# A four-layer token mixer on one core: the comparison of layer 4's weights moves into layer 2's attention and onto GpSimd

## The chip, the cores and the metric

The kernel runs on one core of a Trainium2 chip. The metric is the time of one execution on the device in microseconds, and a kernel is represented by the median of its runs. The engines are named as in the profile: PE (TensorE, with PEld for its weight loads), DVE (VectorE), ACT (ScalarE), POOL (GpSimd) and SP (SyncE, which issues the transfers).

## The reference

Four sequences of 1024 tokens with 256 features pass through four blocks, each followed by a residual sum and a layer norm. The change touches the second block, here called layer 2:

```
q, k   = x @ w_q, x @ w_k                       # 8 heads of 64
gates  = sigmoid(x @ w_gate)                    # 8 experts for each head
gm     = one_hot(argmax(gates)) * gates         # one expert per token and head
values = einsum('bhne,ehdk,bnd->bhnk', gm, value_experts, x)
attn   = softmax(causal(q k^T / 8))
out    = einsum('bhne,ehkd,bhnk->bhnd', gm, output_experts, attn @ values).sum(heads)
```

Layer 4 is a gated feed-forward network whose weights (w1, w2, h1, h2, w3; 128 x 22528 numbers in the layout on the chip) come from the inputs. The kernel copies them to `weights_copy` in DRAM and compares, while layer 2 runs, each number with its value rounded to fp32r. The largest difference goes to `misfit`, and layer 4 leaves out its low-order products where that is zero.

## The kernel before, in words

Layer 2 (`layer2`, line 458) loops over the four sequences, and each turn has three stages, each a block of instructions that all engines finish before the next begins: `values()`, `attention(own, b)` and `output_experts(own, b)`. Engines are synchronised by semaphores. The order on each engine is written out by hand: a number (a tick in the attention, a block in the output stage) runs in the code of every engine, and tables say what happens at which number.

**Attention.** Ticks x run from 8 to 82, eight to a head. In tick x, PE computes the scores of key tile k2 of one head (L902 to L905) into three banks in turn, perhaps a projection (`project`, L659), then the maxima product of query tile k1 of a later head (L886, L888), and last the product of the probabilities with the values of the tick before (L913). ACT takes the exponentials (L944), copies a head's result out (`head_out`, L951) and takes the high parts of a projection (`hi_parts`, four copies). DVE takes the row maxima (L976; the width falls from 1024 to 128 columns over the eight ticks) and then, where a projection stands in the tick, its low parts (`lo_parts`). A pair of heads needs four projections (`parts`: k, k, q, q), which share one bank, so that each waits for the low parts of the one before. In the first five tiles of a head, the maxima product of a tile waits for the row maximum of the tile before. POOL divides six heads by their denominators (L999), which SP carries there and back through DRAM. SP also carries each row maximum to the row that the scores read.

**Output stage.** 64 blocks i (head pair c, expert e, half n; 16 blocks for one c) go through a chain: PE spreads the gates of the block (`mask`, L627), DVE multiplies (`route`, L635), ACT takes the high part (`route_hi`, L642), POOL the low part (`route_lo`, L648), and three blocks later PE does the twelve products (L1176). A ring of four tiles holds the routed blocks. Between these, by number of the block: ACT and DVE split the output experts of the next c into high and low parts (`split_at`; ACT at i, DVE at i + 2), the next sequence is normalised (statistics at block 5, `SD_AT`, `NORM_FROM`, scaling in the eight blocks behind), turned (`turn_at`), its gate logits computed (`LOGITS_AT`, L537) and the gates worked out in ten steps (`GATES_FROM`). The comparison of the weights stands here too: 16 pieces of 128 x 352, each fetched by SP, rounded by ACT (L1103), compared by DVE (L1147) and reduced by DVE (L1152).

## Time and profile before

| what | value |
|---|---|
| runs | 3595.15, 3596.03, 3611.57 us; median 3596.03 |
| the profiled execution | 3602.37 us, span 3600.7 us |
| mean granted clock of TensorE | 0.955 |
| layer 2, four sequences | from 356.2 to about 2004 us |
| PE busy over the span | 3239.3 us (90%) |
| DVE, ACT, POOL busy | 1953.9, 1509.1, 842.4 us |

A row of the timeline gives the start in us, the duration, the engine, the line, the operation with its tiles and shape, how many instructions are merged, and in brackets how long the engine had been idle and what released it. A row of the windows gives the stretch and its length, then the busy time of PE, PEld, DVE, ACT and POOL with the number of instructions, then the granted clock of TensorE (1.00 is 2.4 GHz, 0.50 is 1.2 GHz), the DMA share and GB/s. A row of the groups gives busy us and the mean in ns of one instruction, then the idle time before them and its releaser. The four sequences of layer 2 look alike almost to the tenth of a microsecond, so rows of the first one stand for all.

### The profile page before, as it was taken

What the parts mean: (1) busy time and instruction counts of PE and PEld (TensorE: products, weight loads), DVE (VectorE), ACT (ScalarE), POOL (GpSimd) and SP (SyncE); (2) the same over time, 40 slices, a digit from 0 to 9 for tenths busy, and PEclk for the clock granted to TensorE, in tenths of its full rate; (3) what the DMA queues carried; (4) which work ended last, traced back from release to release, by engine and by line L of the source; (5) the groups of instructions that cost most, each with busy time, mean ns of one, the idle gap of its engine ahead of it and who ended that gap; (6) DMA issues with size and microseconds to landing.
All of it is one profiled execution on the core that took longest, in us unless ns stands there. A gap on an engine that the chain in (4) does not pass through costs nothing. (4 is left out here: it accounts for less than half of the span.)

```text
span 3600.7 us, 50745 instructions
## 1 busy us (share of the span) xinstructions
PE 3239.3 (90%) x18306; PEld 2331.5 (65%) x18306; DVE 1953.9 (54%) x3377; ACT 1509.1 (42%) x2795; POOL 842.4 (23%) x753
## 2 busy tenths in 40 slices
PE   7895999889988999889989698998989979999998
PEld 4554755876568755777558554646556468888887
DVE  4344843867458654677439374765747533333332
ACT  2331144422444134431544455474655634444443
POOL 1121511653037411554027300101000011111111
PEclk9897999999999999999999899999999989999999
DMA  5111100210021100211012101000010030000000
GB/s 190 47 35 66 30 19 13 91 43 24 10 59 49 48 15 16 83 46 30 10 43 64 48 2 26 1 2 25 2 25 2 14 160 12 13 18 12 7 6 12
DMA packets 189927, 127.33 MB, mean 35 GB/s; under 512 B 125808, under 2 KB 174192, under 8 KB 186224
## 3 DMA queue, kind: packets, MB, share of 16 engines
q1 hardware_dynamic: 189680, 124.02, 12.2%
q8 instruction: 157, 2.57, 0.3%
q14 instruction: 90, 0.74, 0.1%
HBM read 106.52 MB, written 28.44 MB: 37 GB/s over the span
## 5 line engine op out<-in xcount | busy, mean ns | idle before, releaser
L1610 ACT ACTIVATE l3b_prob<-sums 128x512 f32<-128x512 f32 (+3 forms) x768 | 332.9, 494 | 207.3 <-PE sums L1543 168.3
L648 POOL TENSOR_TENSOR l_qrow<-l_vm,l_qst 128x512 fp32r<-128x512 f32 x256 | 364.0, 1435 | 205.8 <-ACT l_qst L642 187.0
L1859 PE MATMUL sums<-l_uhi,l_h 128*128 128x512 f32 x1024 | 409.1, 399 | 0.0
L1859 PE MATMUL sums<-l_ulo,l_h 128*128 128x512 f32 x1024 | 403.1, 394 | 0.0
L976 DVE TENSOR_REDUCE l2b_mx<-sums 128x1 fp32r<-128x1024 f32 (+7 forms) x256 | 192.6, 758 | 301.1 <-PE sums L888 299.4
L944 ACT ACTIVATE sb_nx<-sums 128x512 f32<-128x512 f32 (+3 forms) x384 | 181.9, 492 | 355.8 <-PE sums L905 351.2
L913 PE MATMUL sums<-sb_nx,l_vx 128*128 128x512 f32 (+3 forms) x768 | 302.4, 503 | 13.0 <-ACT l_od L951 13.0
L1538 PE MATMUL sums<-l_qst,l_kst 64*128 64x512 f32 (+3 forms) x768 | 276.3, 426 | 21.5 <-DMA l_qst<-l3b_peak 10.9
L1945 DVE TENSOR_TENSOR l_ulo<-l_made,l_uhi 128x512 fp32r<-128x512 f32 x128 | 90.5, 707 | 362.1 <-ACT l_uhi L1876 362.0
L642 ACT CAST l_qst<-l_vm 128x512 fp32r<-128x512 f32 x256 | 157.4, 619 | 240.0 <-DVE l_vm L635 239.6
L1521 PE MATMUL sums<-l_kst,l_qst 64*128 64x512 f32 (+3 forms) x768 | 237.6, 431 | 20.6 <-DVE l3b_low L1622 11.4
L1538 PEld LDWEIGHTS sums<-l_qst,l_kst 64*128 64x128 f32 x768 | 140.3, 195 | 159.0 <-ACT l3b_prob L1610 143.0
L736 PE MATMUL sums<-l_kst,l_qst 128*128 128x512 f32 x512 | 211.2, 412 | 34.5 <-issue 20.6
L635 DVE TENSOR_TENSOR l_vm<-l_oT,sums 128x512 f32<-128x512 f32 x256 | 170.6, 679 | 124.2 <-PE sums L627 123.6
L772 DVE TENSOR_TENSOR l_vm<-sums,l_gm 128x512 f32<-128x512 f32 x256 | 175.0, 689 | 95.2 <-PE sums L736 94.6
L1176 PE MATMUL sums<-l_kst,l_qst 128*128 128x256 f32 x768 | 225.1, 293 | 0.0
L1859 PEld LDWEIGHTS sums<-l_uhi,l_h 128*128 128x128 f32 x1024 | 192.5, 188 | 47.7
L1859 PEld LDWEIGHTS sums<-l_ulo,l_h 128*128 128x128 f32 x1024 | 192.6, 188 | 42.9
L902 PE MATMUL sums<-l_qst,l_kst 128*128 128x512 f32 (+3 forms) x384 | 209.0, 544 | 0.0
L1904 ACT ACTIVATE l_made<-sums,l_scale 128x512 f32<-128x512 f32 x128 | 88.1, 688 | 279.8 <-PE sums L1859 279.7
L736 PE MATMUL sums<-l_kst,l_qrow 128*128 128x512 f32 x512 | 202.6, 396 | 0.0
L736 PE MATMUL sums<-l_krow,l_qst 128*128 128x512 f32 x512 | 202.4, 395 | 0.0
(270 smaller groups left out, 7870.8 us busy)
## 6 DMA issues: line engine op xcount, KB each, us to landing
l_ve<-ve SPq DMA_DIRECT2D x34, 512.0 KB, 4.1
l_oe<-oe SPq DMA_DIRECT2D x16, 1024.0 KB, 6.3
l_vm<-weights_copy SPq DMA_DIRECT2D x64, 176.0 KB, 2.3
sb_nx<-between SPq DMA_DIRECT2D x9, 1024.0 KB, 5.6
weights_copy<-h SPq DMA_DIRECT2D x2, 4096.0 KB, 26.6
l_ve<-inverse SPq DMA_DIRECT2D x32, 256.0 KB, 3.6
l_qst<-l3b_peak SPq DMA_DIRECT2D x512, 0.5 KB, 2.0
l_h<-weights_copy SPq DMA_DIRECT2D x2, 4096.0 KB, 23.6
```

Source lines behind the costliest of these rows:

```text
L648: pool.tensor_tensor(rlo[:, i % RT, :], routed[:, i % RT, :], rhi[:, i % RT, :].bitcast(F32), ALU.subtract).then_inc(s3.routed_lo, 1)
L736: last = pe.matmul(bank(m.ps, n % RING), x[:, c, t * P:(t + 1) * P], v[:, h % 2, c, :], start=(c == 0 and x is xhi and v is vhi), stop=(c ...
L772: dve.tensor_tensor(by_key(vm[:, n % VM, :]), by_key(bank(m.ps, n % RING)), gm[:, at:at + NE].unsqueeze(1).to_broadcast([P, DH0, NE]), ALU ...
L902: pe.matmul(out, kst[:, h % RK, at], qst[:, h % RK, lo:hi], start=True, stop=False)
L913: last = pe.matmul(bank(m.ps, PV, lo, hi), vx[:, k, h // 2, DH0 * (h % 2):DH0 * (h % 2) + P], prob[:, k % 2, lo:hi], start=(k == 0), stop= ...
L944: act.activation(prob[:, k % 2, lo:hi], bank(m.ps, n % 3, 0, hi - lo), ACT.Exp, scale=SCALE0).then_inc(s.exp_ready, 1)
L976: dve.reduce_max(mx[:, h1, t:t + 1], bank(m.ps, max_bank(h1, k1), 0, (t + 1) * P), AX_X).then_inc(s.max_read, 1)
L1176: last = pe.matmul(m.ps[:, t * D:(t + 1) * D], r[:, k % RT, cols], w(c, expert(e))[:, 0, :], start=(c == e == 0 and t % 2 == 0 and r is rh ...
L1521: last = pe.matmul(bank(m.ps, at, 0, hi - lo), qst[rows(a), p, t * P:(t + 1) * P], kst[rows(a), p, lo:hi], start=True, stop=True)
L1538: last = pe.matmul(bank(m.ps, part % SCORE, 0, hi - lo), kst[rows(a), p, k * P:(k + 1) * P], qst[rows(a), p, lo:hi], start=True, stop=True)
L1610: act.activation(prob[:, i % RB, j, a, 0:hi - lo], bank(m.ps, part % SCORE, 0, hi - lo), ACT.Exp, scale=SCALE1).then_inc(s.exp_ready, 1)
L1859: run(lambda out, a, x, first, last: pe.matmul(out, a, x, start=first, stop=last))
```

## The change

- **Comparison.** It leaves the output stage for the attention. There are now eight pieces of 128 x 704 in a sequence. SP fetches two ahead and one more in the second tick of heads 1 to 6; POOL rounds (a cast) and subtracts; DVE takes the result into `worst` by one instruction (not_equal, then max) at the seventh tick of heads 1 to 8. ACT has no part in it. `worst` is reduced to `misfit` once, at the end of the layer. The pieces lie in the tile `vm`, which the attention doesn't use before its last ticks.
- **Projections.** They start at tick 1 of a pair of heads instead of tick 2, so that they stand at odd ticks (k1 = 1, 3, 5, 7) and not at even ones (2, 4, 6, and 0 of the next head).
- **Split of the second pair's output experts.** Blocks 9 and 13 instead of 4 and 8.
- **Statistics.** Four parts of two tiles at blocks 4 to 7, the moments at block 8, where all stood at block 5; the root and the scaling begin two blocks later, as do turns, logits and gates. The last divisions begin one block earlier.

```diff
+    CHECKS = 8
+    W = m.weights_copy.shape[1] // (SEQS * CHECKS)
+    scratch = vm[:, :, :].rearrange("p a n -> p (a n)")
+    word = scratch[:, 0:2 * W].rearrange("p (a n) -> p a n", a=2)
+    rounded, unlike = scratch[:, 2 * W:3 * W].bitcast(F32R), scratch[:, 3 * W:4 * W]
+    worst = sb("worst", [P, W])
...
         WAIT = 2
-        APART = 2
+        PROJECT_FROM, APART = 1, 2
...
         def project_in(x):
-            c, ahead = divmod(x - WAIT, 2 * NT)
+            c, ahead = divmod(x - PROJECT_FROM, 2 * NT)
             if 1 <= c < H0 // 2 and ahead in range(0, 4 * APART, APART):
                 return c, ahead // APART
...
                 sp.dma_start(oe[:, :, :], I["oe2"][:, 0]).then_inc(s.oe_in, 16)
+                sp.wait_ge(m.weights_copied, 16 * len(WEIGHTS4))
+                for j in range(2):
+                    weight_chunk(j)
                 for h in range(H0):
                     if h >= 2:
                         sp.wait_ge(carried[h % 2], carried_to(h - 2))
@@ -856,6 +872,9 @@
                         sp.dma_start(qrow[DH0:ROWS, h % RK, t * P:(t + 1) * P].bitcast(F32),
                                      mx[:, h, t:t + 1].bitcast(F32)).then_inc(carried[h % 2], 16)
                         over = h - 2
+                        if 1 <= h <= CHECKS - 2 and k == CHUNK_AT:
+                            sp.wait_ge(s.weight_unlike, h)
+                            weight_chunk(h + 1)
...
@@ -976,6 +995,9 @@
                         dve.reduce_max(mx[:, h1, t:t + 1], bank(m.ps, max_bank(h1, k1), 0, (t + 1) * P), AX_X).then_inc(s.max_read, 1)
                     if project_in(x):
                         lo_parts(dve, *project_in(x))
+                    if k1 == NT - 2 and h1 >= 1:
+                        dve.wait_ge(s.weight_unlike, h1)
+                        dve.scalar_tensor_tensor(worst[:, :], unlike, 0.0, worst[:, :], ALU.not_equal, ALU.max).then_inc(s.weight_taken, 1)
...
                 pool.memset(krow[DH0:ROWS, :, :].bitcast(F32), -1.0).then_inc(s.row_ready, 1)
+                step = Chain(pool, s.weight_chain)
+
+                def check_weights(j):
+                    pool.wait_ge((s.even_weight_in, s.odd_weight_in)[j % 2], 16 * (j // 2 + 1))
+                    step(pool.tensor_copy(rounded, word[:, j % 2, :]))
+                    if j:
+                        pool.wait_ge(s.weight_taken, j)
+                    pool.tensor_tensor(unlike, word[:, j % 2, :], rounded.bitcast(F32), ALU.subtract).then_inc(s.weight_unlike, 1)
+                    pool.wait_ge(s.weight_unlike, j + 1)
+
+                pool.wait_ge(s.row_ready, 1)
+                check_weights(0)
+                check_weights(1)
                 for h in range(DIVIDED):
+                    if h:
+                        pool.wait_ge(s.o_ready, h)
+                    check_weights(h + 2)
                     pool.wait_ge(s.rden_in, 16 * (h + 1))
                     pool.tensor_tensor(oT[vcol(h), h // 2, :], od[vcol(h), h % 2, :], rden[vcol(h), :], ALU.mult).then_inc(s.o_ready, 1)
...
-        turn_at = {11 + 3 * t: t for t in range(NT)}
-        x_hi_at = {12 + 3 * t: t for t in range(NT)}
-        x_lo_at = {13 + 3 * t: t for t in range(NT)}
-        LOGITS_AT, GATES_FROM, EXP_AT, STATS_AT, SD_AT, NORM_FROM = 35, 37, 38, 5, 6, 7
-        LAST_TURNED, last_o_at = 4, {24: (6, 0), 27: (6, 1), 30: (7, 0), 33: (7, 1)}
-        VALUE_HI_AT, value_lo_at = 48, {49: 0, 51: 1}
+        turn_at = {13 + 3 * t: t for t in range(NT)}
+        x_hi_at = {14 + 3 * t: t for t in range(NT)}
+        x_lo_at = {15 + 3 * t: t for t in range(NT)}
+        LOGITS_AT, GATES_FROM, EXP_AT, MOMENTS_AT, SD_AT, NORM_FROM = 37, 39, 40, 8, 8, 9
+        stats_at = {4: 0, 5: 1, 6: 2, 7: 3}
+        LAST_TURNED, last_o_at = 4, {23: (6, 0), 26: (6, 1), 29: (7, 0), 32: (7, 1)}
+        VALUE_HI_AT, value_lo_at = 51, {53: 0, 55: 1}
         PER_C = NE * NH
         oe_in = (None, s3.oe_in1, s3.oe_in2, s3.oe_in3)
-        split_at = {4: (1, 0), 8: (1, 1)}
+        split_at = {9: (1, 0), 13: (1, 1)}
         split_at.update({(c - 1) * PER_C + 4 + 4 * j: (c, j) for c in range(2, H0 // 2) for j in range(2)})
...
-        CHECKS = 16
-        W = m.weights_copy.shape[1] // (SEQS * CHECKS)
-        word = vm[:, RT:VM, 0:W]
-        rounded = sb("rounded", [P, 2, W], F32R)
-        worst = sb("worst", [P, CHECKS + 1])
-        check_at = {8 + 3 * j: j for j in range(CHECKS)}
-        weight_in = (s3.even_weight_in, s3.odd_weight_in)
...
-                def weight_chunk(j):
-                    if j >= 2:
-                        sp.wait_ge(s.weight_checked, j - 1)
-                    sp.dma_start(word[:, j % 2, :],
-                                 m.weights_copy.rearrange("p (b j n) -> b j p n", b=SEQS, n=W)[b, j]).then_inc(weight_in[j % 2], 16)
...
-                sp.wait_ge(m.weights_copied, 16 * len(WEIGHTS4))
-                for j in range(4):
-                    weight_chunk(j)
                 for c in range(2, H0 // 2):
                     sp.wait_ge(s.oe_lo, 2 * c)
                     sp.dma_start(oe[:, :, :], I["oe2"][:, c]).then_inc(oe_in[c], 16)
-                    for j in range(6 * c - 8, 6 * c - 2):
-                        weight_chunk(j)
                     if c == 2:
                         sp.wait_ge(s.last_o_ready, len(last_o_at))
                         for h in range(2):
@@ -1095,12 +1116,6 @@
...
-                    if i in check_at:
-                        j = check_at[i]
-                        act.wait_ge(weight_in[j % 2], 16 * (j // 2 + 1))
-                        if j >= 2:
-                            act.wait_ge(s.weight_compared, j - 1)
-                        act.copy(rounded[:, j % 2, :], word[:, j % 2, :]).then_inc(s.weight_rounded, 1)
...
-                    if i == STATS_AT:
-                        fetch_stats(dve, m, sf)
+                    if i in stats_at:
+                        part = stats_at[i]
+                        if part == 0:
+                            dve.wait_ge(sf.nx_in, 16)
+                        for t in range(2 * part, 2 * part + 2):
+                            stat = dve.bn_stats(m.stats[:, t, :], m.nx[:, t, :])
+                        stat.then_inc(sf.nx_stats, 1)
+                    if i == MOMENTS_AT:
+                        dve.wait_ge(sf.nx_stats, len(stats_at))
+                        for t in range(NT):
+                            moment = dve.bn_aggr(m.moments[:, t, :], m.stats[:, t, :])
+                        moment.then_inc(sf.nx_moments, 1)
...
-                    if i - 1 in check_at:
-                        j = check_at[i - 1]
-                        dve.wait_ge(s.weight_rounded, j + 1)
-                        dve.wait_ge(weight_in[j % 2], 16 * (j // 2 + 1))
-                        dve.tensor_tensor(word[:, j % 2, :], word[:, j % 2, :], rounded[:, j % 2, :].bitcast(F32),
-                                          ALU.not_equal).then_inc(s.weight_compared, 1)
-                    if i - 2 in check_at:
-                        j = check_at[i - 2]
-                        dve.wait_ge(s.weight_compared, j + 1)
-                        dve.reduce_max(worst[:, j:j + 1], word[:, j % 2, :], AX_X).then_inc(s.weight_checked, 1)
-                dve.wait_ge(s.weight_checked, CHECKS)
-                dve.reduce_max(worst[:, CHECKS:], worst[:, 0:CHECKS], AX_X).then_inc(s.worst, 1)
-                dve.wait_ge(s.worst, 1)
-                dve.tensor_tensor(m.misfit[:, :], m.misfit[:, :], worst[:, CHECKS:], ALU.max).then_inc(s.worst, 1)
                 for t in range(NT):
                     dve.wait_ge(s.out_mm, len(blocks) - (t < NT // 2))
                     dve.tensor_tensor(m.x[:, t, :], m.x[:, t, :], m.ps[:, t * D:(t + 1) * D], ALU.add).then_inc(s.y_ready, 1)
...
+        @block.vector
+        def _(dve):
+            dve.reduce_max(m.misfit[:, :], worst[:, :], AX_X)
```

On DVE in the attention, the rows of the last two projections of a pair (`lo_parts` of the q halves, with the row maxima around them). Before:

```order
L976 TENSOR_REDUCE l2b_mx<-sums 128x1
L982 RECIPROCAL l_denp<-l_denp 128x8
L976 TENSOR_REDUCE l2b_mx<-sums 128x1
L686 TENSOR_TENSOR l_qrow<-sums,l_qst 64x512 x2
L976 TENSOR_REDUCE l2b_mx<-sums 128x1 x2
L686 TENSOR_TENSOR l_qrow<-sums,l_qst 64x512 x2
L976 TENSOR_REDUCE l2b_mx<-sums 128x1 x5
```

Of the changed kernel, at the same place:

```order
L693 TENSOR_TENSOR l_qrow<-sums,l_qst 64x512 x2
L1004 RECIPROCAL l_denp<-l_denp 128x8
L995 TENSOR_REDUCE l2b_mx<-sums 128x1
L1000 SCALAR_TENSOR_TENSOR l_worst<-l_vm,l_worst 128x704
L995 TENSOR_REDUCE l2b_mx<-sums 128x1
L693 TENSOR_TENSOR l_qrow<-sums,l_qst 64x512 x2
L995 TENSOR_REDUCE l2b_mx<-sums 128x1 x6
```

The last low parts stood behind the first row maximum of the next head and now stand ahead of it, and the new `worst` instruction stands between the last two maxima of the head.

On DVE at the start of the output stage, from the third route on. Before:

```order
L635 TENSOR_TENSOR l_vm<-l_oT,sums 128x512 x2
L1124 RECIPROCAL l_denp<-l_denp 128x16
L635 TENSOR_TENSOR l_vm<-l_oT,sums 128x512
L126 BN_STATS sb_stats<-sb_nx 128x6 x8
L130 BN_AGGR sb_moments<-sb_stats 128x2 x8
L1114 TENSOR_TENSOR l_kst<-l_oe,l_krow 128x1024
L635 TENSOR_TENSOR l_vm<-l_oT,sums 128x512 x2
L112 RECIPROCAL sb_rstd<-sb_sd 128x8
```

Of the changed kernel:

```order
L1145 BN_STATS sb_stats<-sb_nx 128x6 x2
L642 TENSOR_TENSOR l_vm<-l_oT,sums 128x512
L1145 BN_STATS sb_stats<-sb_nx 128x6 x2
L642 TENSOR_TENSOR l_vm<-l_oT,sums 128x512
L1145 BN_STATS sb_stats<-sb_nx 128x6 x2
L642 TENSOR_TENSOR l_vm<-l_oT,sums 128x512
L1145 BN_STATS sb_stats<-sb_nx 128x6 x2
L642 TENSOR_TENSOR l_vm<-l_oT,sums 128x512
L1150 BN_AGGR sb_moments<-sb_stats 128x2 x8
L642 TENSOR_TENSOR l_vm<-l_oT,sums 128x512
L112 RECIPROCAL sb_rstd<-sb_sd 128x8
```

The statistics come between the routes in pairs, the low part of an expert half (L1114 before) is gone from here, and the reciprocal of the root follows four routes later.

On POOL in the attention, from the memset of the score rows on. Before, the memset (L996) was followed by the divisions of heads alone. Of the changed kernel:

```order
L1018 MEMSET l_krow 1x4096
L1023 CAST l_vm<-l_vm 128x704
L1026 TENSOR_TENSOR l_vm<-l_vm 128x704
L1023 CAST l_vm<-l_vm 128x704
L1026 TENSOR_TENSOR l_vm<-l_vm 128x704
L1023 CAST l_vm<-l_vm 128x704
L1026 TENSOR_TENSOR l_vm<-l_vm 128x704
L1037 TENSOR_TENSOR l_oT<-l_od,l_ve 64x1024
```

Three pieces are rounded and subtracted ahead of the first head's division (the last row), and one piece stands ahead of each further one.

## Rows read from the trace of the kernel before

**Rows 1.** View by windows, output stage of the first sequence.

```profile
629.00:765.00 136.00, 119.58 (x877) 113.99 (x877) 106.76 (x162) 57.61 (x105) 88.89 (x63) 0.95 0.22 70
```

**Rows 2.** View of waits, 629 to 765 us (us in total, times, longest).

```profile
PE sums L1176 <- POOL l_qrow L648: 11.8, 7, 4.3
```

**Rows 3.** Timeline of PE, output stage; in brackets the idle time before.

```profile
631.11 0.47 PE L627 MATMUL sums<-l_gmT,l_sel 128*128 128x512 f32 x1 [3.17 <-PEq L844]
644.04 0.55 PE L1176 MATMUL sums<-l_ohi,l_qst 128*128 128x256 f32 x1 [4.26 <-POOL l_qrow L648]
721.60 0.55 PE L1176 MATMUL sums<-l_ohi,l_qst 128*128 128x256 f32 x1 [2.59 <-POOL l_qrow L648]
754.79 0.40 PE L627 MATMUL sums<-l_gmT,l_sel 128*128 128x512 f32 x1
756.46 0.40 PE L627 MATMUL sums<-l_gmT,l_sel 128*128 128x512 f32 x1
```

**Rows 4.** Windows with the granted clock (PEclk), three stretches.

```profile
644.00:650.00 6.00, 5.96 (x27) 5.85 (x28) 3.31 (x7) 4.05 (x7) 4.12 (x4) 0.53 0.24 65
721.00:725.00 4.00, 3.40 (x16) 3.34 (x17) 3.93 (x5) 1.19 (x2) 2.10 (x3) 0.57 0.00 0
516.00:520.00 4.00, 4.00 (x14) 1.95 (x12) 0.74 (x1) 1.36 (x3) 0.00 (x0) 1.00 0.04 3
```

**Rows 5.** Groups of instructions by line, 629 to 765 us.

```profile
L648 POOL TENSOR_TENSOR l_qrow<-l_vm,l_qst 128x512 fp32r<-128x512 f32 x63 | 89.6, 1435 | 41.7 <-ACT l_qst L642 37.0 <-PE sums L1176 4.6
L635 DVE TENSOR_TENSOR l_vm<-l_oT,sums 128x512 f32<-128x512 f32 x61 | 40.6, 678 | 18.5 <-PE sums L627 18.4
L642 ACT CAST l_qst<-l_vm 128x512 fp32r<-128x512 f32 x61 | 37.6, 620 | 59.9 <-DVE l_vm L635 59.8
L1147 DVE TENSOR_TENSOR l_vm<-l_vm,l2c_rounded 128x352 f32<-128x352 f32 x16 | 20.4, 1273 | 2.7 <-ACT l2c_rounded L1103 2.3
L537 PE MATMUL sums<-l_wg,l_xT 128*128 128x64 f32 x32 | 3.7, 273 | 0.0
```

**Rows 6.** Timeline of DVE and ACT, blocks 4 to 7.

```profile
637.93 2.71 DVE L126 BATCH_NORM_STATS2 sb_stats<-sb_nx 128x6 f32<-128x256 f32 x8 [0.78 <-DMA sb_nx<-between]
640.45 1.04 ACT L1081 CAST l_krow<-l_oe 128x1024 fp32r<-128x1024 f32 x1 [7.49 <-DMA l_oe<-oe]
644.02 1.28 ACT L136 ACT_TABLE_LOAD   x1
```

**Rows 7.** Timeline of ACT and DVE, blocks 36 to 40.

```profile
706.63 1.05 ACT L1081 CAST l_krow<-l_oe 128x1024 fp32r<-128x1024 f32 x1 [4.15 <-DMA l_oe<-oe]
712.17 0.72 DVE L554 TENSOR_SCALAR l_od<-l_od 128x512 f32<-128x512 f32 x1 [2.03 <-ACT l_od L543]
713.97 3.34 DVE L557 RECIPROCAL l_od<-l_od 128x512 f32<-128x512 f32 x1
```

**Rows 8.** Timeline of PE, attention of the first sequence.

```profile
515.64 1.10 PE L913 MATMUL sums<-sb_nx,l_vx 128*128 128x512 f32 x2 [1.37 <-ACT l_od L951]
528.33 0.22 PE L886 MATMUL sums<-l_kst,l_qst 128*128 128x128 f32 x1
530.55 1.98 PE L659 MATMUL sums<-l_xT,l_wq 128*128 128x512 f32 x4 [0.65 <-DVE l_qrow L686]
534.37 0.68 PE L886 MATMUL sums<-l_kst,l_qst 128*128 128x512 f32 x2 [0.37 <-DVE l2b_mx L976]
537.52 0.61 PE L886 MATMUL sums<-l_kst,l_qst 128*128 128x512 f32 x2 [0.84 <-DVE l2b_mx L976]
```

**Rows 9.** Timeline of DVE, the same place in the attention.

```profile
533.09 1.23 DVE L976 TENSOR_REDUCE l2b_mx<-sums 128x1 fp32r<-128x1024 f32 x1 [2.28 <-PE sums L888]
534.96 1.39 DVE L686 TENSOR_TENSOR l_qrow<-sums,l_qst 64x512 fp32r<-64x512 f32 x2 [0.64 <-ACT l_qst L674]
536.38 1.09 DVE L976 TENSOR_REDUCE l2b_mx<-sums 128x1 fp32r<-128x896 f32 x1
```

**Rows 10.** Groups by line, attention of the first sequence, 456 to 629 us.

```profile
L987 DVE TENSOR_TENSOR l_kst<-l_oe,l_ohi 128x1024 fp32r<-128x1024 f32 x2 | 2.4, 1218 | 0.0
```

11 lines of the change are left out of this document (8 added, 3 removed).

## The prediction

> **What bounds the kernel now.** I read the table of engines first: PE is busy for 90% of the span, and the four layers run one after the other, so what layer 2 saves comes off the end one for one. The windows by stage then show the output stage as the place where PE does not run freely: in 136 us it is busy for 119.6, at a granted clock of 0.95 [rows 1]. The waits of that stretch put 11.8 us of PE's idle time down to POOL's low parts, 7 times, the longest 4.3 us [rows 2]; POOL itself waits for ACT and ACT for DVE, so the chain route, high part, low part is late, and not an engine that is full.
>
> The timeline gives the size. Block 3's mask starts at 631.11 and block 63's at 756.46, which is 125.35 us for 60 blocks; at the end a block takes 1.67 us [rows 3], and 60 of those are 100.2. So 25.1 us are above the pace. The logits take 3.6 of it (3.7 us busy, partly overlapped) [rows 5] and stay. The largest event is at 644.04, where PE has stood for 4.26 us [rows 3] and then runs at a mean clock of 0.53 for 6 us [rows 4], which costs 6 x 0.47 = 2.8 more: 7.1 us. The second is at 721.60: 2.59 idle [rows 3], then 4 us at 0.57 [rows 4], 1.7: 4.3 us. The other waits for POOL are 11.8 - 4.26 - 2.59 = 4.9. The rest, 25.1 - 3.6 - 7.1 - 4.3 - 4.9 = 5.2, is the half clock after the start, the turns and small delays; I leave it as it is, but for 1 us.
>
> In the attention PE's rows have few gaps. A pair of heads shows 0.65 before the fourth projection, then 0.37 and 0.84 before maxima, and 1.37 before the values product that waits for ACT's copy of a head [rows 8]; the 0.37 comes twice. That is 3.6 us a pair. After the 1.37 the clock stays at 1.00 [rows 4].
>
> **Split at block 9.** What stops PE at 644.04 is ACT, which at block 4 waits 7.49 us for the output experts' transfer [rows 6], with the high parts behind it. The transfer lands at 640.45. At block 9 ACT arrives later than that: masks then run at 1.67 from block 5 at about 636, so block 9 is at 642.7. The wait is gone. What is late next is DVE: the statistics now stand at block 4, and the sequence's rows land only at 637.93 [rows 6]. Route 5 waits for that, 637.93 + 0.68 for a quarter of the 2.71 us = 638.6. Route, high part and low part take 0.68 + 0.62 + 1.30 (1.435 with the contention of the mean) [rows 5], so low part 5 is ready at 641.3. PE wants it in block 8, at 641.3. No stall, but no slack.
>
> **Root and scaling at blocks 9 and 10.** Each route now shares its turn with 0.68 of statistics: 1.36 of 1.67 us. The moments end at 644.05. ACT then loads a table (1.28 [rows 6]) and takes the root, until 645.6, and splits the experts (1.04 [rows 6]) ahead of high part 9: low part 9 is ready at 648.6 and PE wants it at 648.1. DVE's reciprocal chain, 2.5 us as before, puts route 10 at 648.1 and low part 10 at 651.7, as the expert's low part (1.22 [rows 10]) falls into it; PE wants that at about 650.2. Stalls: 0.4 + 1.5 = 1.9, and 0.2 for what follows, 2.1 us, each too short for the clock by the 1.37 that left it alone. Gain here: 7.1 - 2.1 = 5.0. From both sides: nothing new in its place gives 7.1; if DVE's wait and the chain together stop PE as long as ACT did, 0.
>
> **The comparison leaves the output stage.** DVE loses 16 instructions of 1.27 us [rows 5] and 16 reductions of some 0.5, about 28.5 us of 136. ACT loses 16 casts. The four short waits (4.9) stand where one of those 1.27 us fell beside an expert's low part or an x part. Without them DVE has about 1 us in a block to spare, and the chain of 2.6 to 2.8 us has 1.95 until PE's 5.25 (three blocks and a mask) less POOL's queue. A low part of 1.2 to 2.3 then fits. I take 0.5 left of 4.9: gain 4.4.
>
> **Blocks 36 to 46.** SP can fetch the last pair's experts only behind the last divisions, so ACT's wait of 4.15 at block 36 [rows 7] stays; now the logits (block 37) lie over it wholly, where they stood one block ahead of it. DVE waits 2.03 for ACT's exponential, then takes a reciprocal of 3.34 [rows 7]. That pair stays, two blocks later, and an expert's low part (1.22) now stands just ahead of the reciprocal: route 42 is 1.9 late, which the slack takes, and route 43 is 0.68 + 3.34 after it, 4.2 late. That leaves PE a wait of 4.2 - 1.95 = 2.2 against 2.59, and the clock may fall again (1.7). Gain 0.4, or 2.1 if the clock holds. I take 1.2.
>
> Output stage: 5.0 + 4.4 + 1.2 + 1 for the small delays = 11.6 us a sequence. Bounds: 7 (the second and third at half) to 16.
>
> **Projections at odd ticks.** Before, the fourth one started at 530.55, and its low parts ended at 534.96 + 1.39 = 536.35 [rows 9], 5.80 later. Only the next maximum but one was behind it, as the 1024-wide maximum had gone ahead at 533.09. Now this maximum (1.23 [rows 9]) stands behind the low parts, and the maxima product of the next tick waits for it: 5.80 + 0.03 + 1.23 + 0.06 = 7.1 after the start of the projection. PE has in between what lay from 530.55 to 534.00 (3.45, the 0.37 taken off) and one tick more, 528.33 to 529.90 (1.57) [rows 8]: 5.0. So the 0.65, one 0.37 and the 0.84 become one wait of 2.1. The first projection of the pair comes to lie in the other 0.37, which goes. It also leaves the tick of ACT's copy: 2.35 us of copies were ahead of it, so the 1.37 goes. The second projection waits 0.2 for the low parts of the first (5.75 against 5.6 of PE's work). A pair: 3.6 - 2.3 = 1.3. The first pair has no head to copy out: 0.6. Sum 3.2 a sequence. Bounds: 0.84 kept and the rest gone gives 8; 12 waits with the clock's 1.7 each give -2.
>
> **The comparison in the attention.** POOL: a subtraction of 704 is 1.435 x 704/512 = 1.97 at most [rows 5]; a cast has no row, between nothing and the same; a division at most 2.9 by that rate. Some 6.9 us of a head's 22 us, beside nothing that waits. DVE: eight instructions with two SBUF inputs, 1.218 x 704/1024 = 0.84 [rows 10]. Each stands behind the 256-wide maximum, and DVE is idle there for 1.3 us before the last one of the head, so they cost 0. Without that cover it would be 8 x 0.84 = 6.7 a sequence. SP waits for `weight_unlike` at tick 1 of a head; the subtraction it needs comes two ticks (some 4 us) earlier. Behind that wait stand the maxima's carries, needed eight ticks later. POOL's divisions are due eleven ticks later. All nothing.
>
> The Trainium skill, "GPSIMD Engine Reference", Key points, says that GpSimd shares its SBUF interfaces with VectorE and that a VectorE instruction with two SBUF inputs contends for them. The comparison before shows that (1.27 us for 352 columns, where 1024 columns of another such instruction took 1.22 [rows 5, 10]). By it the new instruction would suffer if it ran beside the cast. In the order of the program its subtraction is over and the next waits for it, and the cast is some ticks old, so I expect no overlap; the opposite is a rival below.
>
> **Sum.** (11.6 + 3.2) x 4 = 59 us. The profiled execution took 3602.37 (6.3 above the median of the runs), so it would be 3543, and the median 3596 - 59 = 3537.
>
> **Rivals.**
> - *The clock falls behind the new waits of 2.1 us in the attention.* For it: 2.59 did it [rows 3, 4]; against: 1.37 did not. 12 x 1.7 = 20: 3557. Chance 0.2.
> - *Statistics and root take over the stall of block 4.* For it: no slack at route 5. The 5.0 is lost four times, 20: 3557. Chance 0.08.
> - *The worst instruction meets POOL's cast.* It would wait up to 2.0; less 1.3 of cover, 0.7 x 8 x 4 = 22: 3559. Against: the order. Chance 0.05.
> - *The stage comes down to its pace:* 4 more a sequence, 16: 3521. Chance 0.1.
> - *No change:* the comparison was hidden anyway and all waits are replaced, 3596. Against: the rows of waits. Chance 0.04.
> - *Slower: POOL holds SP up.* If cast, subtraction and division took longer than a head's 22 us, SP's wait would set the head's pace: at 25, 3 x 7 pieces x 4 = 84 less 59, 3621. It decides above 24 us of POOL's work in a head, against 6.9. Chance 0.03.
> - The forecast itself: 0.5, by its own terms 3525 to 3550.
>
> **Numbers.** 3537, range 3518 to 3562, which holds the first four rivals and the forecast. Half a per cent, 18 us, is what a measurement of this kernel tells from no change. Faster by more (below 3578): 0.93; within: 0.04; slower: 0.03.
>
> **What would show it.** Right: no wait of ACT for the experts before block 9; PE's 4.26 replaced by waits of at most 2; mask 3 to mask 63 in about 114 us; about 2.1 before the second maxima product of each head that follows four projections, and no wait for the copied head with a projection ahead; the worst instruction at about 0.84. Wrong: a half clock in the attention three times a sequence, routes 5 to 11 that stop PE for over 3 us together, the worst instruction above 1.3 or POOL's cast above 5, or a reciprocal that stops PE for longer than 2.6.

## The result, and the profile of the changed kernel

The changed kernel takes 3547.07 us (median of four runs, 3544.36 to 3559.71) against 3599.55 us of the kernel before (3595.15 to 3611.57, with the one run that was added to those shown). The ratio is 0.9856 with a 95% interval of 0.9821 to 0.9891: 52 us less, where 59 were predicted, and inside the range.

The page of the profiled execution gives a span of 3558.0 us, 42.7 less than before.

```profile
span 3558.0 us, 50502 instructions
PE 3244.9 (91%) x18306; PEld 2338.8 (66%) x18306; DVE 1906.2 (54%) x3274; ACT 1491.9 (42%) x2731; POOL 912.5 (26%) x818
```

Layer 2 saved more than that: its last row on DVE starts at 1949.3 us, and at 2002.4 before, which is 53.1 us. Some of it was given back in layer 3, which the change doesn't touch. The row of one of its products shows it by its last two times, the first and the last start: 796.0 us apart here, 781.1 (2078.4 to 2859.5) in the execution before.

```profile
L1536 PE MATMUL sums<-l_kst,l_qst x768: 216/436/793, 2022.5 to 2818.5; 64*128 64x512 f32 x128, 64*128 64x128 f32 x32, 64*128 64x384 f32 x32
```

This profiled execution was the slowest of the four; so the whole is read from the runs, and the stages of layer 2 from the traces. (The four sequences are alike in their waits, but not in the clock: a short fall of the clock, or none, makes most of the difference between them, so all four are read below.)

**Output stage.** The timeline of PE, at the places that answer to [rows 3]. The first and the last row are the masks of blocks 3 and 63.

```profile
629.83 0.68 PE L634 MATMUL sums<-l_gmT,l_sel 128*128 128x512 f32 x1 [3.17 <-PEq L851]
652.04 0.36 PE L1187 MATMUL sums<-l_ohi,l_qst 128*128 128x256 f32 x1 [1.20 <-POOL l_qrow L655]
659.84 0.36 PE L1187 MATMUL sums<-l_ohi,l_qst 128*128 128x256 f32 x1 [0.67 <-POOL l_qrow L655]
672.76 0.35 PE L1187 MATMUL sums<-l_krow,l_qst 128*128 128x256 f32 x1 [0.56 <-POOL l_qrow L655]
714.46 0.35 PE L1187 MATMUL sums<-l_ohi,l_qst 128*128 128x256 f32 x1 [1.60 <-POOL l_qrow L655]
744.23 0.40 PE L634 MATMUL sums<-l_gmT,l_sel 128*128 128x512 f32 x1
```

From mask to mask it is 114.40 us (125.35 before), and 113.2 to 113.3 in the other three sequences. The stop of 4.26 us is gone; in its place stand 1.20, 0.67 and 0.56 ahead of the products of blocks 11, 15 and 22 (0.73, 0.67 and 0.57 in the other three sequences). Behind the reciprocal, ahead of block 43, stands 1.60, where 2.59 stood. In the means of four sequences the stage had 12.2 us of PE's waits and 12.8 us at 1.2 GHz before; now it has 3.7 and 6.2. With half of the slow time counted as lost, 106.8 us are left in both kernels, so these two explain the gain of 11.9. The view of waits, 629 to 757 us, answers to [rows 2]:

```profile
PE sums L1187 <- POOL l_qrow L655: 4.0, 4, 1.6
ACT l_krow L1102 <- DMA l_oe<-oe: 3.5, 1, 3.5
DVE sb_stats L1145 <- DMA sb_nx<-between: 2.3, 1, 2.3
```

POOL's low parts hold PE up for 4.0 us in all instead of 11.8. ACT still waits for the last pair's experts (3.5 us, block 36), and DVE for the statistics' rows (2.3 us, block 4), and neither shows on PE.

On DVE, a step of the normalising chain (before, then changed), the low part of an expert half and the reciprocal:

```profile
646.46 1.21 DVE L114 SCALAR_TENSOR_TENSOR sb_sd<-sb_moments,sb_eps,sb_sd 128x8 f32<-128x8 f32 x1
644.52 0.23 DVE L114 SCALAR_TENSOR_TENSOR sb_sd<-sb_moments,sb_eps,sb_sd 128x8 f32<-128x8 f32 x1
646.96 2.32 DVE L1129 TENSOR_TENSOR l_kst<-l_oe,l_krow 128x1024 fp32r<-128x1024 f32 x1
708.23 3.35 DVE L563 RECIPROCAL l_od<-l_od 128x512 f32<-128x512 f32 x1
```

The third step of the chain (L114) now takes 0.23 us where it took 1.21 beside POOL; the expert's low part takes 2.32 beside POOL, against 1.22 alone [rows 10]. The reciprocal is as long as before [rows 7].

**Attention.** The timeline of PE, the rows that answer to [rows 8]; the first is the start of the first scores, the last ACT's copy of a head:

```profile
466.52 0.47 PE L921 MATMUL sums<-l_qst,l_kst 128*128 128x512 f32 x1 [1.02 <-issue]
533.16 0.50 PE L905 MATMUL sums<-l_kst,l_qst 128*128 128x512 f32 x1 [2.22 <-DVE l2b_mx L995]
1334.12 0.68 PE L905 MATMUL sums<-l_kst,l_qst 128*128 128x512 f32 x2 [2.24 <-DVE l2b_mx L995]
614.49 1.10 PE L932 MATMUL sums<-sb_nx,l_vx 128*128 128x512 f32 x2 [0.52 <-ACT l_od L970]
```

The one wait of 2.2 us in a pair is there twelve times out of twelve, between 2.21 and 2.24. The waits of 1.37 are gone; the 0.52 of the last heads was there before. New is the wait of 1.02 us ahead of the first scores ("issue": nothing that the profile names released it). The granted clock (third number from the right) behind two of the waits of 2.2 us:

```profile
534.00:537.40 3.40, 3.40 (x13) 2.44 (x11) 1.35 (x2) 1.19 (x2) 1.97 (x2) 0.55 0.20 20
1334.00:1340.00 6.00, 5.88 (x28) 3.81 (x28) 2.94 (x4) 2.98 (x5) 2.98 (x2) 1.00 0.25 63
```

After the first the clock stands mostly at 1.2 GHz, after the second at 2.4. In ten of the twelve cases it fell. What a fall costs can be read in the same trace: from one such wait to the next, a pair of heads takes 43.8 to 43.9 us where the clock fell for 3.4 us, 42.3 to 42.4 where it did not, and 45.3 where it fell for 6.8. A short fall is 1.6 us. Before, every pair took 44.2.

The comparison's own instructions (durations in ns as least/median/greatest, and first and last start; the rows without a line number say who waited):

```profile
L1000 DVE SCALAR_TENSOR_TENSOR l_worst<-l_vm,l_worst x32: 877/882/893, 482.6 to 1811.6; 128x704 f32<-128x704 f32 x32
  POOL l_vm L1026: 395.5, 28
L1023 POOL CAST l_vm<-l_vm x32: 769/770/772, 461.6 to 1798.5; 128x704 fp32r<-128x704 f32 x32
L1026 POOL TENSOR_TENSOR l_vm<-l_vm x32: 1671/1683/1689, 462.4 to 1807.7; 128x704 f32<-128x704 f32 x32
```

DVE's instruction takes 0.88 us, 0.89 at most, and never meets POOL's cast or division; POOL waits 395.5 us for it in 28 cases and has that time.

### The profile page after: what moved, and what is told of

The parts are those of the page before. It is cut to its first block and busy times, and to the rows that moved or that the text cites. A ratio compares the mean times of both kernels' runs of the same rounds, so it can differ in the third digit from the quotient of the medians.

```text
span 3558.0 us, 50502 instructions
## 1 busy us (share of the span) xinstructions
PE 3244.9 (91%) x18306; PEld 2338.8 (66%) x18306; DVE 1906.2 (54%) x3274; ACT 1491.9 (42%) x2731; POOL 912.5 (26%) x818
## 3 DMA queue, kind: packets, MB, share of 16 engines
q1 hardware_dynamic: 185072, 124.02, 12.2%
## 5 line engine op out<-in xcount | busy, mean ns | idle before, releaser
L655 POOL TENSOR_TENSOR l_qrow<-l_vm,l_qst 128x512 fp32r<-128x512 f32 x256 | 354.8, 1398 | 166.9 <-ACT l_qst L649 144.5
L1553 PE MATMUL sums<-l_qst,l_kst 64*128 64x512 f32 (+3 forms) x768 | 284.0, 437 | 23.6 <-DMA l_qst<-l3b_peak 13.4
L1536 PE MATMUL sums<-l_kst,l_qst 64*128 64x512 f32 (+3 forms) x768 | 252.1, 453 | 15.7 <-DVE l3b_low L1637 7.2
```

The lines of the kernel that those rows point to most:

```text
L655: pool.tensor_tensor(rlo[:, i % RT, :], routed[:, i % RT, :], rhi[:, i % RT, :].bitcast(F32), ALU.subtract).then_inc(s3.routed_lo, 1)
L1536: last = pe.matmul(bank(m.ps, at, 0, hi - lo), qst[rows(a), p, t * P:(t + 1) * P], kst[rows(a), p, lo:hi], start=True, stop=True)
L1553: last = pe.matmul(bank(m.ps, part % SCORE, 0, hi - lo), kst[rows(a), p, k * P:(k + 1) * P], qst[rows(a), p, lo:hi], start=True, stop=True)
```

## The experiments

The stages of layer 2 in every kernel, worked out from the timeline of PE. The attention is the time from its first maxima product to the mask of block 3, the output stage from that mask to the one of block 63; us, four sequences each. What varies within a row is for the most part whether the clock falls once more or less; b_odd's output stage, in which nothing is changed, is 1.7 off, so differences below 2 us are read together with the rows of waits. The last column is the whole time: the median where there were several runs (changed, a_even, a_chunks_behind, a_late, a_all and the kernel before), else the one run. The kernel before ran beside them on the same chips at medians of 3608.29, 3599.98 and 3602.70.

| kernel | attention | mean | output stage | mean | whole |
|---|---|---|---|---|---|
| before | 175.6 174.0 173.9 175.6 | 174.8 | 125.4 126.0 125.2 125.2 | 125.4 | 3599.55 |
| b_no_compare | 174.0 175.6 175.6 175.6 | 175.2 | 117.2 119.3 118.8 119.5 | 118.7 | 3575.80 |
| b_split9 | 175.7 174.0 175.6 175.6 | 175.2 | 125.9 124.2 125.8 126.0 | 125.5 | 3612.20 |
| b_no_compare_split9 | 174.0 174.0 173.9 175.6 | 174.4 | 115.3 115.4 115.3 116.5 | 115.6 | 3561.24 |
| b_tables | 175.6 173.9 175.6 174.0 | 174.8 | 123.9 123.0 123.6 123.7 | 123.6 | 3589.48 |
| b_odd | 172.4 174.0 173.9 172.4 | 173.2 | 125.3 126.7 128.6 127.8 | 127.1 | 3607.40 |
| changed | 174.1 172.5 174.3 174.4 | 173.8 | 114.4 113.3 113.2 113.2 | 113.5 | 3547.07 |
| a_even | 178.6 176.8 177.1 176.9 | 177.3 | 114.5 113.0 113.4 113.0 | 113.5 | 3567.31 |
| a_split4 | 172.5 175.7 172.8 174.1 | 173.7 | 117.5 116.8 116.8 116.7 | 117.0 | 3558.05 |
| a_no_compare | 172.5 174.0 173.9 172.4 | 173.2 | 113.3 113.2 113.1 113.2 | 113.2 | 3548.16 |
| a_chunks_behind | 172.4 174.0 172.4 174.1 | 173.2 | 113.1 114.4 113.3 113.0 | 113.4 | 3544.98 |
| a_take1 | 176.2 179.6 176.4 178.1 | 177.6 | 113.1 113.0 113.1 113.1 | 113.1 | 3563.80 |
| a_late | 165.3 165.1 165.0 165.0 | 165.1 | 114.5 114.3 114.4 114.4 | 114.4 | 3516.59 |
| a_all | 165.0 165.0 165.0 165.0 | 165.0 | 112.2 112.1 112.2 112.1 | 112.2 | 3507.67 |

### b_no_compare: the kernel before without the comparison

```diff
-        check_at = {8 + 3 * j: j for j in range(CHECKS)}
+        check_at = {}
...
-                for j in range(4):
-                    weight_chunk(j)
...
-                    for j in range(6 * c - 8, 6 * c - 2):
-                        weight_chunk(j)
...
-                dve.wait_ge(s.weight_checked, CHECKS)
-                dve.reduce_max(worst[:, CHECKS:], worst[:, 0:CHECKS], AX_X).then_inc(s.worst, 1)
-                dve.wait_ge(s.worst, 1)
-                dve.tensor_tensor(m.misfit[:, :], m.misfit[:, :], worst[:, CHECKS:], ALU.max).then_inc(s.worst, 1)
```

> The kernel before with the comparison of layer 4's weights left out altogether (nothing is fetched, rounded or compared; misfit stays zero). Own theory: the late chain in the output stage was made late by the comparison's sixteen contended VectorE instructions, so the short waits of PE for POOL (4.9 us a sequence) shrink to about 0.5 while the 4.26 at block 4 and the wait behind the reciprocal (2.6) stay: mask 3 to mask 63 in about 120 us instead of 125.35. Rival: the comparison was hidden, and the waits come from the experts' low parts and the x parts alone: 124 us or more.

The stage took 118.7 us, 6.7 less than before. On the timeline of PE the waits of 0.82 and 1.78 us ahead of blocks 22 and 26 are gone, the stop that follows ACT's wait at block 4 is as it was, and 1.92 stays behind the reciprocal (2.59 before):

```profile
642.35 0.36 PE L1168 MATMUL sums<-l_ohi,l_qst 128*128 128x256 f32 x1 [4.21 <-POOL l_qrow L648]
714.98 0.35 PE L1168 MATMUL sums<-l_ohi,l_qst 128*128 128x256 f32 x1 [1.92 <-POOL l_qrow L648]
```

The comparison was not hidden. It cost 6.7 us a sequence (27 us in all), more than the 4.9 of short waits that the prediction put down to it. PE's waits account for 5.2 of the 6.7 (12.2 us before, 7.0 here, means of four); 0.7 of that is the wait behind the reciprocal, which the comparison had also made longer.

### b_split9: the kernel before with the later split alone

```diff
-        split_at = {4: (1, 0), 8: (1, 1)}
+        split_at = {9: (1, 0), 13: (1, 1)}
```

> The kernel before with the second pair's experts split at blocks 9 and 13 instead of 4 and 8, and nothing else. Own theory: ACT's wait for the transfer is the whole cause of the 4.26 us stop and of the half clock behind it, so it goes, about 7 us less less some 1 to 2 for the root at block 7, which no longer has the stop to hide in: mask 3 to mask 63 in 119 to 120 us. Rival: the root and the table load at block 6 and 7 stop PE as long by themselves: 123 us or more.

Mask to mask took 125.5 us (3612.20 on the whole): nothing gained, and the own theory is refuted as it was put. The stop of 4.26 us is gone from the timeline of PE. In its place stand four waits ahead of blocks 8, 11, 13 and 14 (1.08, 1.46, 0.53, 0.55; the first two below); the late waits are unchanged (the last row is the one behind the reciprocal):

```profile
650.51 0.36 PE L1176 MATMUL sums<-l_ohi,l_qst 128*128 128x256 f32 x1 [1.08 <-POOL l_qrow L648]
657.43 0.35 PE L1176 MATMUL sums<-l_ohi,l_qst 128*128 128x256 f32 x1 [1.46 <-POOL l_qrow L648]
723.22 0.35 PE L1176 MATMUL sums<-l_ohi,l_qst 128*128 128x256 f32 x1 [2.58 <-POOL l_qrow L648]
```

The rival named the root and the table load; the rows speak for a third reading. The waits stand behind the blocks in which the scaling, the experts' low parts and the comparison now fall together. The stop had been the time in which DVE did such work for nothing. In all, PE waits 12.4 us a sequence (12.2 before).

### b_no_compare_split9 and b_tables: what the split needs

The first is b_no_compare with the split at 9 and 13. The second is the kernel before with all tables of the changed output stage, the comparison left in it:

```diff
-        split_at = {4: (1, 0), 8: (1, 1)}
+        split_at = {9: (1, 0), 13: (1, 1)}
...
-        LOGITS_AT, GATES_FROM, EXP_AT, STATS_AT, SD_AT, NORM_FROM = 35, 37, 38, 5, 6, 7
+        LOGITS_AT, GATES_FROM, EXP_AT, MOMENTS_AT, SD_AT, NORM_FROM = 37, 39, 40, 8, 8, 9
+        stats_at = {4: 0, 5: 1, 6: 2, 7: 3}
```

> The kernel before without the comparison and with the split at blocks 9 and 13. The split alone brought nothing beside the comparison, the comparison alone left the 4.2 us stop. Theory of the shared slack: the split works once VectorE has room in blocks 8 to 18, so the stop goes, the small waits behind it stay below 2.5 us together, and mask 3 to mask 63 takes 113 to 115 us. Rival: the statistics in one piece and the root at block 7 keep 4 us or more of waits: 117 or more.

> The kernel before with all tables of the changed output stage (split at 9 and 13, statistics spread, root, turns, logits, gates and divisions moved), while the comparison stays in the stage. Theory of the shared slack: about as the split alone, 122 to 125 us from mask 3 to mask 63. Rival, spreading the statistics is what makes room: 119 or less.

Without the comparison the split brings 3.1 us (118.7 to 115.6), above the foretold 115 by 0.6. The small waits did not stay below 2.5 us either: where the stop of 4.21 was, 0.93, 0.22, 1.09 and 1.03 stand ahead of blocks 6, 7, 8 and 11 of the first sequence, 3.3 together. PE's waits in the stage fell by only 1.0 (7.0 to 6.0, means of four), and the time at 1.2 GHz fell from 12.0 to 4.3 us. So most of what the split brings is the clock, which fell behind the stop and behind none of these waits of about 1. With the comparison, all tables together bring 1.8 (125.4 to 123.6), within what was expected, but no more than b_odd's stage is off. From 115.6 to the 113.5 of the changed kernel are the spread statistics and the other tables, 2.1, again near that bound. Taking the comparison out of a stage with the new tables brings 123.6 - 113.5 = 10.1, taking it out of the old one 6.7: the edits add more together than apart. That they share one slack, that of DVE and of the chain behind it, is the reading that fits these numbers and the rows of waits.

### a_split4: the changed kernel with the early split

The diff is that of b_split9, the other way round.

> The changed kernel with the split back at blocks 4 and 8. Theory: ACT waits for the transfer again, PE stops for about 4 us with the half clock behind it, and the small waits at blocks 12 to 18 go: mask 3 to mask 63 in 117.5 to 119.5 us instead of 113.3, 17 to 25 us on the whole. Rival: the statistics at blocks 4 to 7 hide the transfer and the stage keeps 114.

117.0 us, 3.4 more than the changed kernel and half a microsecond below the range. The stop is there again, at 3.50 us on the timeline of PE:

```profile
642.74 0.55 PE L1187 MATMUL sums<-l_ohi,l_qst 128*128 128x256 f32 x1 [3.50 <-POOL l_qrow L655]
```

The split that waits for the transfer is the cause of the stop: the stop goes and comes with it in both kernels. In this surrounding its removal is worth 3.4 us a sequence and not 5.0.

### b_odd and a_even: the projections apart

b_odd is the kernel before with `divmod(x - 1, 2 * NT)` in `project_in`; a_even is the changed kernel with `PROJECT_FROM = 2`.

> The kernel before with the projections at odd ticks, and nothing else. From the profile of the changed kernel: a wait of 2.2 us once in each pair in place of 0.65, 0.37, 0.84, one 0.37 and 1.37, followed by the half clock in most pairs. Own theory now: the attention (first maxima product to block 3's mask) takes 172.5 to 174.5 us against 174 to 175.6 before, so the odd ticks bring 0 to 1.5 us a sequence. Rival: without the comparison's VectorE instruction the wait of 2.2 is shorter and they bring 3 us.

> The changed kernel with the projections back at even ticks 2, 4, 6 and 0 of the next head; all else stays. Own theory: the waits of before return (3.6 us a pair in small pieces) and the half clock goes, so a sequence's attention takes 174 to 175.6 us, 0 to 1.5 more than in the changed kernel; the time is 3547 to 3553. Rival: the comparison's instruction in the attention, behind the low parts at even ticks, costs more there than at odd ticks (its cover of idle time is smaller), and the attention takes over 178 us: above 3560.

b_odd: 173.2 us in the attention, 1.6 below the kernel before (a shade above the 0 to 1.5 expected, and far from the rival's 3), with three waits of 2.23 us: the wait is no shorter without DVE's new instruction. Again the clock fell behind ten of twelve of them. The whole time, 3607.40 us, does not show the gain. a_even: 177.3, 3.5 above the changed kernel, and 3567.31 us (3561.82 to 3577.97) on the whole, a ratio of 0.99 (0.9864 to 0.9935) to the kernel before. That is above what the own theory said; the whole is above 3560, as the rival had it, and the attention below its 178 us. The small waits of the pairs are the same 0.65, 0.37, 0.84 and 1.37 to the hundredth as in [rows 8], and a pair takes the same 44.2 us as before, so the instruction of the comparison isn't what costs. The loss lies in the first 20 us: by the twelfth of the attention's maxima products it is 2.6 us behind the kernel before (mean of four), and at the stage's end 2.5. The timeline of PE at the first scores of a_even, and the window behind it:

```profile
468.09 0.77 PE L921 MATMUL sums<-l_qst,l_kst 128*128 128x512 f32 x1 [1.43 <-issue]
468.00:472.00 4.00, 3.91 (x8) 2.31 (x9) 0.00 (x0) 1.19 (x2) 0.00 (x0) 0.50 0.37 94
```

The first scores wait 1.43 us (1.11 to 1.32 in the other sequences) and then run at half clock, in all four sequences; before they waited for nothing, and the clock fell there in two of four. The scores need the row maxima of head 0, which SP carries. The last line of the view by tile (`l_qrow`, the first 20 us of the attention) gives the time from issue to landing of these carries, least, median and greatest; of the changed kernel first, then of a_chunks_behind, below:

```profile
DMA to landing us min/median/max: 1.9/3.5/4.9
DMA to landing us min/median/max: 1.9/2.0/3.5
```

In the kernel before the median was 1.9 us, in a_even 3.7. The two first pieces of the weights, 352 KB each, are issued ahead of the carries, behind the experts' 1 MB. That they are the cause at even ticks too is argued from this; no kernel with even ticks moved them.

### a_no_compare and a_chunks_behind: the cost of the comparison in the attention

a_no_compare leaves the comparison out of the changed kernel (no fetch, cast, subtraction or DVE instruction). a_chunks_behind moves the two first fetches:

```diff
-                for j in range(2):
-                    weight_chunk(j)
                 for h in range(H0):
...
+                        if h == 0 and k == NT - 1:
+                            weight_chunk(0)
+                            weight_chunk(1)
                         if 1 <= h <= CHECKS - 2 and k == CHUNK_AT:
```

> The changed kernel with the comparison left out altogether (no fetch, no cast, subtraction or VectorE instruction in the attention; misfit stays zero). Theory after the first four runs: the comparison costs the attention through its first two transfers, which lie ahead of the carries of head 0's row maxima and hold the first scores up by 1 us; the rest of it is free. So a sequence's attention is 0 to 2 us shorter than in the changed kernel (172.4 to 174.4) and the carries of head 0 land in 1.9 us instead of 3.5. Rival: the VectorE instruction and POOL's work cost all along the stage: 3 us shorter or more.

> The changed kernel with the first two pieces of the weights fetched behind the carries of head 0 instead of ahead of them. Theory of the transfers: the wait of PE before the first scores (0.8 to 1.3 us) goes or halves, the carries land in 1.9 us again, and the attention equals that of the kernel without a comparison; the whole time falls by 2 to 8 us against the changed kernel. Rival, the comparison's instructions: no change in the attention.

Both take 173.2 us in the attention, against 173.8 of the changed kernel. With the fetches behind, the carries land as fast as without a comparison, PE's wait ahead of the first scores (0.81 to 1.26 us in the four sequences) is gone, and the whole takes 3544.98 us (3541.46 to 3547.57), a ratio of 0.9843 (0.9828 to 0.9858), which is within the error of the changed kernel's.

The 0.6 us must not be read as the price of the transfers. By the twelfth maxima product of the attention only 0.2 us are left of the wait of 1 us (mean of four); the rest of the 0.6 is the changed kernel's one long fall of the clock. The same move between a_late and a_all, below, where the clock doesn't vary, changes the attention from 165.1 to 165.0. So at odd ticks the comparison costs 0.2 us a sequence or less, and the wait for the carries is nearly all covered by what follows it. At even ticks it costs 2.5 (177.3 against 174.8), where no projection fills the time ahead of the first scores: about 1.3 of wait, and the clock's fall in four sequences instead of two. DVE's instruction and POOL's work are free where they stand.

### a_take1: the place of DVE's instruction

```diff
-                    if k1 == NT - 2 and h1 >= 1:
+                    if k1 == 1 and 1 <= h1 <= H0:
```

> The changed kernel with VectorE's instruction of the comparison behind the 896-wide maximum of a head (second tick, heads 1 to 8) instead of behind the 256-wide one. Theory of the cover: the instruction (0.88) is free only where VectorE idles. In the second tick of a head PE's next maxima product waits for the maximum ahead of it, which is read before the instruction, so part of 0.88 shows only where the next maximum starts late: 0 to 0.9 us for each of 7 heads, 1 to 5 us a sequence. Rival: no place on VectorE costs anything, attention unchanged within 0.5 us.

177.6 us in the attention, 3.8 more. That is inside the range of the cover, and the rival falls, but the range was met by luck: the missing cover is the smaller part of it. On the timeline of PE a maxima product waits 1.58 us for a maximum where there was no wait before (first row), and on DVE and POOL the same place shows why:

```profile
602.31 0.56 PE L905 MATMUL sums<-l_kst,l_qst 128*128 128x512 f32 x2 [1.58 <-DVE l2b_mx L995]
598.59 2.80 DVE L1000 SCALAR_TENSOR_TENSOR l_worst<-l_vm,l_worst 128x704 f32<-128x704 f32 x1
598.25 2.39 POOL L1037 TENSOR_TENSOR l_oT<-l_od,l_ve 64x1024 f32<-64x1024 f32 x1 [14.64 <-DMA l_ve<-inverse]
```

This one instruction, head 7's, falls beside POOL's division and takes 2.80 us instead of 0.88 (2.76, 2.70 and 2.72 in the other sequences). Up to there the kernel is only 0.4 us behind the changed one in the first sequence (in the others the clock's falls stand between), and directly behind it 2.1; in three of the four sequences the clock falls behind the new wait of 1.5 besides, 1.6 us more. The other seven take 0.88 to 0.89 here, but for one of 1.05 and one of 1.16 (first two sequences). The 0.4 us came as 0.2 at each of two heads in which the next maximum follows without a pause of DVE. So the missing cover costs 0.4 us, and the one meeting with POOL, with the clock behind it, most of the rest of the 3.8. Behind the 256-wide maximum the instruction never meets POOL.

### a_late: the low parts behind the wide maximum

```diff
                     if project_in(x):
-                        lo_parts(dve, *project_in(x))
+                    for at, held in ((x, False), (x - 1, True)):
+                        if project_in(at) and (project_in(at)[1] == 3) == held:
+                            lo_parts(dve, *project_in(at))
```

> The changed kernel with one thing moved: VectorE takes the low parts of a pair's fourth projection one tick later, behind the 1024-wide row maximum of the next head. Theory of the wait of 2.2 us: it is the low parts that stand ahead of that maximum. The wait falls to 0.4 before the second maxima product, with one of about 0.4 before the third, 1.4 us less, three times a sequence, and the half clock that follows 9 of the 12 waits goes with it (up to 1.7 each). Attention 168 to 170.5 us, the whole 15 to 25 us faster than the changed kernel. Rival: the low parts are only late themselves, the third maxima product waits as long, and nothing is gained.

165.1 us in the attention, 8.7 less than in the changed kernel, and 3516.59 us on the whole (3512.95 to 3520.9), a ratio of 0.9763 (0.9748 to 0.9778): 30 us less than the changed kernel, more than expected. On DVE the 1024-wide maximum now starts ahead of the low parts (the first row), and PE's second maxima product waits 0.37 us (the last row, of PE):

```profile
528.20 1.23 DVE L995 TENSOR_REDUCE l2b_mx<-sums 128x1 fp32r<-128x1024 f32 x1 [1.53 <-PE sums L907]
529.34 1.38 DVE L693 TENSOR_TENSOR l_qrow<-sums,l_qst 64x512 fp32r<-64x512 f32 x2
530.75 1.09 DVE L995 TENSOR_REDUCE l2b_mx<-sums 128x1 fp32r<-128x896 f32 x1
529.48 0.67 PE L905 MATMUL sums<-l_kst,l_qst 128*128 128x512 f32 x2 [0.37 <-DVE l2b_mx L995]
```

No third product waits for its maximum, so the rival falls. A pair of heads now takes 40.9 us, every time, where the changed kernel has 42.3 without a fall of the clock and 43.9 with one. So about 1.45 us of the 1.85 that the wait became shorter reach the stage, three times a sequence (4.3 us); the rest, some 4.4 us, is the clock, which fell behind ten of the twelve waits of the changed kernel (the expectation says nine: a miscount), 1.6 us for a short fall, and behind none here.

### a_all: both moves and the reciprocal in halves

```diff
-                lambda: step(dve.reciprocal(g[:, :], z[:, :])),
+                lambda: step(dve.reciprocal(g[:, 0:N // 2], z[:, 0:N // 2])),
+                lambda: step(dve.reciprocal(g[:, N // 2:], z[:, N // 2:])),
```

> The changed kernel with both moves (the low parts behind the wide maximum, the first pieces behind the carries) and the reciprocal of the gates in two halves of 256 columns in two blocks. Theory: route 43 is late by one half (1.7 us) instead of 3.35, so PE's wait of 1.6 behind the reciprocal goes, with the half clock after it: mask 3 to mask 63 in 110.5 to 111.5 us instead of 113.3. With the two moves in the attention the whole is 25 to 40 us faster than the changed kernel, a ratio of 0.975 to 0.98 to the kernel before. Rival: the halves make the gates late for something else and the stage keeps 113.

3507.67 us (3503.08 to 3516.24), a ratio of 0.9746 (0.973 to 0.9762): 39 us less than the changed kernel, and the best of all. The wait behind the reciprocal fell from 1.60 to 0.48 (the first row of PE's timeline, below). The stage took 112.2 us, not 110.5 to 111.5: the expectation also counted on the half clock behind the 1.60, but in the changed kernel the clock fell there in one of four sequences only, so there was the wait alone to gain, 1.1 us. (Against a_late, where it fell in all four, the stage gained 2.2.) In the first sequence a wait of 1.59 stands near the beginning, ahead of block 5 (the second row); the last two rows are the windows from block 3's mask on in the first and in the second sequence:

```profile
706.22 0.36 PE L1190 MATMUL sums<-l_ohi,l_qst 128*128 128x256 f32 x1 [0.48 <-POOL l_qrow L656]
631.16 0.36 PE L1190 MATMUL sums<-l_ohi,l_qst 128*128 128x256 f32 x1 [1.59 <-POOL l_qrow L656]
620.70:626.60 5.90, 5.86 (x45) 5.75 (x46) 1.54 (x3) 1.24 (x2) 2.60 (x2) 1.00 0.56 158
1009.60:1015.50 5.90, 5.88 (x27) 5.71 (x28) 1.54 (x3) 1.24 (x2) 1.98 (x2) 0.53 0.58 171
```

The statistics at block 4 wait for their rows, and at full clock PE comes to block 5's products before the low part does: the place that the prediction called without slack. In the other three sequences the stage begins at half clock, the wait isn't there, and the stage takes the same 112.1 to 112.2 us. Either of the two is paid there.

## Why the prediction was right, and where it was off

- **The sum.** 59 us against 52 by the runs and 53 by layer 2 in the traces. The output stage gave 11.9 us a sequence, where 11.6 were predicted; the attention gave 0.95, where 3.2 were. Another 0.4 lies between the stages.
- **Split at block 9.** The cause was right: the stop is the transfer's (a_split4). Its term, 5.0, was too large: 3.4 in the changed kernel, 3.1 without the comparison, and nothing in the kernel before (b_split9). The prediction took it as a term of its own; it is one only once the comparison is gone, and then most of it is the clock.
- **The comparison leaves the output stage.** Predicted 4.4; taken out alone it gave 6.7, and out of a stage with the new tables 10.1. This term was too small about by what the other was too large. That their sum, 11.6, came out at 11.9 is luck in its parts. The rows of single waits did not tell it; only kernels with one edit each do.
- **Root and scaling.** 2.1 us of waits were predicted, ahead of blocks 9 and 10; 1.20 + 0.67 = 1.87 came (1.40 in the other sequences), ahead of blocks 11 and 15, each behind a low part of an expert half. The 0.56 ahead of block 22 stands where 0.82 stood and answers to the 0.5 that was left for the short waits. The chain on DVE was shorter (1.1 us instead of 2.5), as POOL stood still, and the expert's low part longer (2.32 instead of 1.22): two errors that came near to cancelling.
- **Reciprocal.** 2.2 predicted, 1.60 measured. The half clock that was left open came in the first sequence, where mask to mask went up to 4.15 and then 2.63 us; in the other three it was 3.6 and 1.7.
- **Odd ticks.** The wait of 2.1 us was foretold and is 2.2, in every pair; the 1.37 went. The waits alone gave more than predicted: a pair without a fall of the clock went from 44.2 to 42.3 us, 1.9 where 1.3 was predicted. What failed is the term that the prediction put at nothing: that the clock falls behind the new wait was a rival with 0.2, at 1.7 us for each of twelve. It happened in ten of twelve, at 1.6 for a short fall, which is why 0.95 was left of 3.2. The price was right, and so was the bound of 2.59 that had done it. The bound on the other side was not: "1.37 did not" was read from one place, and the same trace has a fall behind a wait of 1.32 at the first head, in two of the four sequences:

```profile
464.30 0.68 PE L886 MATMUL sums<-l_kst,l_qst 128*128 128x512 f32 x2 [1.32 <-DVE l2b_mx L976]
464.00:468.00 4.00, 3.70 (x10) 2.28 (x11) 1.34 (x2) 1.19 (x2) 0.00 (x0) 0.66 0.06 4
```

- **The comparison in the attention.** "All nothing" holds for DVE, POOL and SP's wait. It failed for the transfers: the two pieces ahead of head 0's carries were counted as issues and not as traffic. They made PE wait 0.8 to 1.3 us ahead of the first scores, of which 0.2 us a sequence or less reach the stage here; at even ticks 2.5 us were lost at that place. The price of the instruction without cover, 8 x 0.84 = 6.7 us, is far too high for the other place that was tried: in a_take1 seven of the eight instructions cost 0.4 us together.
- **Contention of DVE's instruction with the cast** (a rival with 0.05): 0.88 us at the median and 0.89 at most, so it did not occur in the changed kernel. It is a live danger all the same: in a_take1, which moves the instruction, it took 2.70 to 2.80 us beside POOL's division, which the prediction had not named as a partner, and an expert's low part, an instruction with two SBUF inputs, took 2.32 us beside POOL in the trace of the changed kernel. The rule of the Trainium skill, "GPSIMD Engine Reference", Key points, that such an instruction contends with GpSimd, agrees with both.

## What to carry to other kernels

In a chain of engines that runs close to its pace, edits that free the same slack can't be priced apart: remove each alone, and together, before giving it a share of the sum. When work moves into an idle engine, look at its first transfers too: with 0.7 MB ahead of half-kilobyte carries PE waited for its first scores, about 1 us each time, which one order of ticks covered and the other did not. A stage that costs what was expected isn't yet the mechanism that was expected: look which instruction grew. Of two engine queues that feed each other, ask at each place which instruction stands ahead of the one that PE waits for; here one exchange on DVE was worth 30 us, more than half of the whole change.
